# A five-stage attention and RWKV pipeline on one core: additions moved from GpSimd's datapath into accumulating DMA transfers, and a new order of the jobs

## The chip, the core and the metric

The kernel runs on one core of a Trainium2 chip. A core has five engines that run their own instruction streams and wait for each other by semaphores: TensorE (PE), VectorE (DVE), ScalarE (ACT), GpSimd (POOL) and SyncE (SP); 16 DMA engines move data. The metric is the device time of one launch in microseconds, the median of the runs. The kernel before: 1928.44 us (three runs, 1928.34 to 1928.8).

## The reference

32 samples of 128 x 512 floats pass two blocks, each with the second input `ctx_2048` beside it. The first takes a sample as 128 channels by 512 positions (`conv1x1` is a product with a 128 x 128 matrix and a bias, `inorm` a normalisation over the positions):

```python
Mn = conv1x1(Wn, bn, inorm(x_c));  Mm = conv1x1(Wm, bm, inorm(x_s))
A  = softmax(einsum('bct,bcs->bts', Mn, Mm))
x  = conv1x1(Wo, bo, einsum('bcs,bts->bct', conv1x1(Wl, bl, x_s), A)) + x_c
```

The second is an RWKV block (embedding E = 512, H = 32 heads of 16, sequence 128):

```python
xa = ln(x);  sx = concat(state[:, 1:2] - xa[:, :1], xa[:, :-1] - xa[:, 1:])
xxx = einsum(tanh((xa + sx * maa_x) @ maa_w1), maa_w2)      # five mixings
xk, xw, xv, xr, xg = xa + sx * (maa_stack + xxx)            # the sum that the change moves
w = exp(-exp(time_decay + tanh(xw @ td_w1) @ td_w2))
r, k, v = xr @ Wr.T, xk @ Wk.T, xv @ Wv.T;  g = silu(xg @ Wg.T)
for t: a = k_t v_t^T;  out_t = r_t (u * a + s);  s = a + w_t * s
x1 = x + groupnorm(out) * g @ Wo.T
xc = ln(x1);  xk2, xr2 = xc + sx2 * ffn_maa_k, xc + sx2 * ffn_maa_r
return x1 + sigmoid(xr2 @ Wfr.T) * (relu(xk2 @ Wfk.T)**2 @ Wfv.T)   # and this last sum
```

## The kernel before, in words

The work on it is cut into jobs, and the program is 36 steps of software pipelining: in step s every engine works on up to five samples at once, `b0` (sample s, attention), `b1` (mixing and projections), `b2` (the recurrence), `b3` (group norm, output projection, second layer norm), `b4` (feed-forward end). The order of the jobs on each engine is written out by hand in the five `step` functions; nothing is reordered at run time. A job waits for semaphore counts (`Steps.count`) of the jobs that it needs, then the engine goes on with the next one in its list. PSUM banks are dealt out in a ring by the order in `FRONT_JOBS` and `BACK_JOBS`.

The recurrence of one sample is eight units on DVE, `wkv_outer` (the product of `vrep` and `kT` into `S`, L595), `wkv_scan` (L604) and `wkv_read` (L613). After each unit PE sums over the state, `wkv_sum` (L1101). `S` and `vrep` have two buffers, so the outer product of unit u waits for the sum of unit u - 2; POOL copies the initial state of a unit into `S` (`wkv_s0`, L446), also after the sum of unit u - 2. SP loads `vrep` (512 KB, from DRAM, with each row repeated for 16 partitions) once a unit.

The mixing goes: PE multiplies (`mid_M`, L1057), ACT adds the stack in PSUM (`mid_bias`, L806), DVE multiplies by `sx` into `xf` (`mid_mix`, L570), POOL adds `xa` into `xf` (`mid_add`, L430), and PE projects `xf` (`mid_P`, L974: `Wv`, `Wk`, `Wr`, `Wg`; `mid_D1`, L1078, for w). `xf` has three buffers for the five mixings, in the order v, w, k, r, g. At the end of a sample DVE multiplies into `rr` (`fin_y`, L668), POOL adds `x1` (`fin_out`, L460) and ACT's queue stores `rr` (`fin_store`). POOL also computes the reciprocal roots (`rstd_of`, L400 and L402; the one on `hrs` takes longest) and the product `rku` (`wkv_rk`, L436).

Of the kernel before, what the change touches and what calls it, by code (L numbers as in the profile page):

```python
# [18 lines left out]
ALU = mybir.AluOpType  # L19
# [54 lines left out]
def run(step):  # L74
# [7 lines left out]
    "Mn:0 Mm:0 W1:1 S0:0 Wt:1 S1:0 S2:0 Mv:1 Mw:1 S3:0 Mk:1 Mr:1 Vp:1 Mg:1 D1:1 V:0 T0:0 T1:0 "  # L82
    "T2:0 T3:0 D2:1 E2:1 O:0 Kp:1 Rp:1 G:1 Tx:0").split())]
BACK_JOBS = [(j, int(lag)) for j, lag in (x.split(":") for x in (
    "FV:4 Tg:3 Wo:3 Tx2:3 FK:3 C:2 FR:3").split())]
# [3 lines left out]
def build(nc, x_c, x_s, state, params, att_w, big_w, maa_w1, maa_w2, td_w1, td_w2, out, v_dram):  # L89
    with ExitStack() as ctx:  # L90
# [109 lines left out]
        v_stored = sem("v_stored")  # L200
        out_stored = sem("out_stored")
# [10 lines left out]
        dve_att = Steps(sem("dve_att"), "stats aggr nm mx0 mx1 mx2 ri0 mx3 ri2 ri1 ri3 xin xst xag nm1")  # L212
        dve_mid = Steps(sem("dve_mid"), "sx xx mv mw mk mr s0m s0c mg g")
# [3 lines left out]
        act_att = Steps(sem("act_att"), "xn yn Mn Mm p0 p1 p2 n0 n1 p3 n2 n3 v T0 T1 T2 T3 xhat")  # L217
        act_mid = Steps(sem("act_mid"), "xa tn tx vT dt ez k th r")
        act_mix = Steps(sem("act_mix"), "bv bw br bk bg")
# [56 lines left out]
        def _(sp):  # L276
# [64 lines left out]
            def step(s, on):  # L341
                b0, b1, b2, b3, b4 = on
                if b0: load_st1(b0[0], b0[2])
                if b2: load_vrep(b2[0], b2[2], 4)
                if b2: load_vrep(b2[0], b2[2], 5)
                if b0 and b0[0] + 1 < NB: load_x(b0[0] + 1, 1 - b0[2])
                if b2: load_vrep(b2[0], b2[2], 6)
                if b2: load_vrep(b2[0], b2[2], 7)
                if b1: load_vrep(b1[0], b1[2], 0)
                if b1: load_st0(b1[0], b1[2])  # L350
                if b1: copy_xres(*b1)
                if b1: load_vrep(b1[0], b1[2], 1)
# [8 lines left out]
        def _(eng):  # L361
# [54 lines left out]
            def mid_xa0(n, m, p):  # L416
                v0 = held(eng, regs[0], 16 * (m + 1))
                v1 = held(eng, regs[1], dve_mid.count("xx", n - 1))
                v2 = held(eng, regs[2], pool_mid.count("fg", n - 1))
# [3 lines left out]
                eng.wait_ge(pool_mid.sem, v2)  # L423
# [34 lines left out]
            def fin_out(n, m, p):  # L458
                eng.wait_ge(dve_fin.sem, dve_fin.count("y", n))
                po.tensor_tensor(rr[:, :], rr[:, :], x1[:, :], ALU.add).then_inc(pool_fin.sem, 1)  # L460

            def step(s, on):
                b0, b1, b2, b3, b4 = on
                if b3: wkv_s0(*b3, 6)
                if b4: tail_xc20(*b4)
                if b2: mid_add(*b2, 4)
                if b3: wkv_s0(*b3, 7)
                if b1: att_rstd1(*b1)
                if b1: mid_xa0(*b1)
# [20 lines left out]
        def _(eng):  # L490
# [35 lines left out]
            def att_xin(n, m, p):  # L526
# [25 lines left out]
            def mid_shift(n, m, p):  # L552
# [3 lines left out]
                                  ALU.subtract).then_inc(dve_mid.sem, 1)  # L556
                eng.wait_ge(dve_mid.sem, dve_mid.count("sx", n))
# [21 lines left out]
            def mid_s0(n, m, p):  # L579
# [3 lines left out]
                ve_.tensor_reduce(s0m[:, :], s, X, ALU.add).then_inc(dve_mid.sem, 1)  # L583
                eng.wait_ge(dve_mid.sem, dve_mid.count("s0m", n))
# [59 lines left out]
            def tail_x1(n, m, p):  # L644
                eng.wait_ge(pe_tail.sem, pe_tail.count("Wo", n))
                eng.wait_ge(xres_copied[p], 16 * (m + 1))
                eng.wait_ge(pool_fin.sem, pool_fin.count("out", n - 1))
                ve_.tensor_tensor(x1[:, :], bank_of("Wo")[:, :], xres[:, p, :], ALU.add).then_inc(dve_tail.sem, 1)
                eng.wait_ge(dve_tail.sem, dve_tail.count("x1", n))
                ve_.bn_stats(st62[:, :], x1[:, :]).then_inc(dve_tail.sem, 1)  # L650
                v0 = held(eng, regs[0], dve_tail.count("st", n))
# [18 lines left out]
            def step(s, on):  # L670
                b0, b1, b2, b3, b4 = on
                if b3: wkv_read(*b3, 7)
                if b1: att_rstd1(*b1)

                if b2: wkv_outer(*b2, 0)
                if b0: att_stats(*b0)
                if b2: wkv_scan(*b2, 0)
                if b2: mid_gate(*b2)
                if b2: wkv_read(*b2, 0)
                if b0: att_rstd(*b0)  # L680

# [9 lines left out]
                if b0: att_max(*b0, 0)  # L691
# [561 lines left out]
```

## Time and profile before

| | |
|---|---|
| median of the runs | 1928.44 us |
| the profiled execution's own time | 1927.65 us |
| its span, first to last instruction | 1925.7 us |
| busy, share of the span: PE, DVE | 94%, 93% |
| busy: ACT, POOL | 63%, 57% |
| chain that ended last: DVE, issue, PE, POOL | 54%, 28%, 8%, 8% |
| mean granted TensorE clock | 0.973 |

A busy share is an average over the span, with the filling and draining of the pipeline in it. An instruction's duration runs from its start to its end; the next one on the same engine can begin a little before that end, so for the pace of an engine the starts are compared. A number in brackets at the end of a row is the time the engine was idle before it, and what ended it.

### The profile page before, as it was taken

Reading aid. Unit: us, or ns where it says so; the run is one execution under the profiler, and the core shown is the slowest. Engines: PE = TensorE matmul, PEld = TensorE weight load, DVE = VectorE, ACT = ScalarE, POOL = GpSimd, SP = SyncE. Lnnn points to the kernel's source line nnn. Section 1 sums busy time; section 2 is a strip of 40 time slices with the busy share of each in tenths; the row PEclk is TensorE's granted clock in tenths of the full one; section 3 lists DMA queues with packets and bytes.
Section 4 is the critical chain, followed back from the end, with each engine's and each line's share of the span. In section 5 each row is a group of like instructions: output and inputs, shape, how many; then the busy total and the mean of one; then the engine's idle time right before and its main releaser. Section 6 shows DMA issues by size and latency. Waiting matters only on the chain.

```text
span 1925.7 us, 34674 instructions
## 1 busy us (share of the span) xinstructions
PE 1811.8 (94%) x12356; PEld 1254.5 (65%) x12356; DVE 1785.9 (93%) x2084; ACT 1206.5 (63%) x2849; POOL 1104.6 (57%) x822
## 2 busy tenths in 40 slices
PE   5889999999999999999999999999999999999855
PEld 2666666677666667766666677667667766766633
DVE  3599999999999999999999999999999999999871
ACT  3545766666676666667666666766666666665422
POOL 1256666656666665666666556666655665655431
PEclk8889999999999999999999999999999999999877
DMA  6233333334333333434333343334333333433310
GB/s 236 63 95 97 99 98 97 93 101 106 105 102 98 101 90 101 105 102 106 97 103 92 100 104 102 102 99 103 91 99 105 102 103 96 105 84 95 93 49 11
DMA packets 86202, 189.31 MB, mean 98 GB/s; under 512 B 18800, under 2 KB 35312, under 8 KB 85008
## 3 DMA queue, kind: packets, MB, share of 16 engines
q1 hardware_dynamic: 64528, 170.32, 33.2%
q10 hardware_dynamic: 21504, 16.78, 2.8%
q8 instruction: 100, 1.64, 0.4%
q14 instruction: 70, 0.57, 0.1%
HBM read 161.91 MB, written 16.78 MB: 93 GB/s over the span
## 4 chain that ended last, share of the span: by engine, by line
DVE 54%; issue 28%; PE 8%; POOL 8%; ACT 1%; DVEq 0%; DMA 0%; POOLq 0%; ACTq 0%; SPq 0%
DVE S L604 17%; DVE S L595 11%; POOL hrs L400 4%; DVE S L613 3%; PE bank L974 3%; DVE xr L663 3%; POOL hrs L402 2%; DVE xf L570 2%; POOL S L446 2%; DVE xx L560 2%; PE bank L981 1%; DVE st L532 1%; DVE st L650 1%; DVE xin L529 1%; DVE sx L555 1%
## 5 line engine op out<-in xcount | busy, mean ns | idle before, releaser
L604 DVE TENSOR_TENSOR_SCAN S<-wrep,S 128x1024 f32<-128x1024 f32 x256 | 588.4, 2298 | 2.7 <-ACT wrep L842 0.8
L446 POOL COPY S<-s 128x8 f32<-128x8 f32 x256 | 181.4, 709 | 497.0 <-PE bank L1101 496.8
L430 POOL TENSOR_TENSOR xf<-xf,xa 128x512 f32<-128x512 f32 x160 | 335.2, 2102 | 30.8 <-DVE xf L570 29.1
L595 DVE TENSOR_TENSOR S<-vrep,kT 128x1016 f32<-128x1016 f32 x256 | 337.4, 1318 | 1.3 <-ACT kT L825 1.3
L613 DVE TENSOR_TENSOR S<-S,rT 128x1024 f32<-128x1024 f32 x256 | 316.1, 1235 | 2.3
L806 ACT ACTIVATE bank<-bank,par 128x128 f32<-128x128 f32 x640 | 179.0, 352 | 150.0 <-PE bank L1057 150.0
L400 POOL TENSOR_SCALAR rstd<-mv 128x1 f32<-128x1 f32 (+1 forms) x96 | 129.0, 1344 | 154.7 <-DVE mv L536 83.2
L1101 PE MATMUL bank<-S,slide 128*32 128x256 f32 x2048 | 167.1, 398 | 46.9 <-DVE S L613 46.9
L402 POOL TENSOR_TENSOR hrs<-hrs,mhalf 128x32 f32<-128x32 f32 x32 | 177.4, 5542 | 2.7
L757 ACT ACTIVATE xhat<-xin,nmr,rstd 128x512 f32<-128x512 f32 x32 | 26.1, 815 | 210.5 <-DVE nmr L502 210.5
L1008 PE MATMUL bank<-probT 128*128 128x512 f32 x256 | 134.9, 611 | 7.6 <-ACT prob L769 6.8
L842 ACT ACTIVATE wrep<-ez 128x1016 f32<-128x1016 f32 x128 | 133.3, 1043 | 0.0
L974 PEld LDWEIGHTS bank<-xk,Wfk 128*128 128x128 f32 x1024 | 121.0, 197 | 17.3 <-issue 13.2
L974 PE MATMUL bank<-xk,Wfk 128*128 128x128 f32 x1024 | 127.1, 284 | 3.8 <-DVE xk L663 3.8
L974 PEld LDWEIGHTS bank<-xf,Wk 128*128 128x128 f32 x1024 | 118.6, 194 | 13.6 <-issue 13.6
L400 POOL TENSOR_SCALAR hrs<-hvar 128x32 f32<-128x32 f32 x32 | 69.5, 2171 | 100.7 <-DVE hvar L631 100.7
L886 ACT ACTIVATE xp<-bank,prev 128x128 f32<-128x128 f32 x256 | 127.1, 496 | 0.0
L974 PE MATMUL bank<-xf,Wv 128*128 128x128 f32 x1024 | 126.3, 284 | 0.0
L974 PEld LDWEIGHTS bank<-xf,Wg 128*128 128x128 f32 x1024 | 116.7, 192 | 12.8 <-issue 12.8
L981 PE MATMUL bank<-Wo,ogT 128*128 128x512 f32 x256 | 122.7, 623 | 2.4 <-DVE ogT L642 2.4
L974 PE MATMUL bank<-xf,Wk 128*128 128x128 f32 x1024 | 124.5, 281 | 0.0
L974 PEld LDWEIGHTS bank<-xf,Wv 128*128 128x128 f32 x1024 | 123.4, 201 | 1.3 <-issue 1.0
(133 smaller groups left out, 3770.1 us busy)
## 6 DMA issues: line engine op xcount, KB each, us to landing
vrep<-v_dram SPq DMA_DIRECT2D x256, 512.0 KB
xc<-x_c SPq DMA_DIRECT2D x32, 256.0 KB, 6.4
xs<-x_s SPq DMA_DIRECT2D x32, 256.0 KB, 7.1
v_dram<-vT ACTq DMA_DIRECT2D x32, 256.0 KB, 6.1
xres<-xin SPq DMA_DIRECT2D x32, 256.0 KB, 5.9
out<-rr ACTq DMA_DIRECT2D x32, 256.0 KB, 6.3
Wv<-big_w SPq DMA_DIRECT2D x1, 1024.0 KB, 7.4
Wk<-big_w SPq DMA_DIRECT2D x1, 1024.0 KB, 9.4
```

The costliest lines, as they stand in the source:

```text
L400: po.tensor_scalar(rs, var, EPS, None, ALU.add).then_inc(own.sem, 1)
L402: po.tensor_tensor(rs, rs, mhalf[:, 0:rs.shape[1]], ALU.pow).then_inc(own.sem, 1)
L430: po.tensor_tensor(xf[:, b, :, :], xf[:, b, :, :], xa[:, :, 1:P + 1], ALU.add).then_inc(pool_mid.sem, 1)
L446: po.tensor_copy(S[:, u % 2, :, 0], s0[:, p, k:k + UJ]).then_inc(pool_wkv.sem, 1)
L595: ve_.tensor_tensor(S[:, u % 2, :, 1:P], vrep[:, u % 2, :, 0:P - 1], k, ALU.mult).then_inc(dve_wkv.sem, 1)
L604: ve_.tensor_tensor_scan(s, wrep[:, u % C, :, :].rearrange("p j t -> p (j t)"), s, 0.0, ALU.mult, ALU.add).then_inc(dve_wkv.sem, 1)
L613: ve_.tensor_tensor(s, s, rT[:, p, u % C, :].unsqueeze(1).broadcast_to([P, UJ, P]), ALU.mult).then_inc(dve_wkv.sem, 1)
L806: last = sc.activation(ps, ps, ACT.Identity, bias=col("maa_stack", c, MIX.index(f)))
L974: last = pe.matmul(ps[:, o * P:(o + 1) * P], w[:, c, o * P:(o + 1) * P], src[:, c, :], start=(c == 0), stop=(c == C - 1))
L981: last = pe.matmul(bank_of(job)[:, :], src[:, c, :], w[:, c, :], start=(c == 0), stop=(c == C - 1))
L1008: pe.matmul(bank_of(f"S{t}")[:, :], Mn[:, t * P:(t + 1) * P], Mm, start=True, stop=True).then_inc(pe_att.sem, 1)
L1101: last = pe.matmul(bank[SUM_BANK][32 * g:32 * g + 32, 2 * P * half:2 * P * (half + 1)], ones, S[:, u % 2, g:UJ:4, :], start=(c == 0), stop ...
```

## The change

1. `mid_add` and `fin_out` are no longer POOL tensor instructions. Each is a DMA issued from POOL's queue with `accum_op=ALU.add`, from `xa` into `xf` (five a sample) and from `x1` into `rr` (one a sample). Each kind has a semaphore of its own (`xa_added[f]`, `x1_added`), which counts 16 for a landed transfer.
2. Whoever waited for POOL's counter waits for these: PE's projections and `D1`, ACT's `mid_xa` (for all five, before it overwrites `xa`), DVE's `tail_x1` and ACT's `fin_store` (for the last addition).
3. Functions that issued two or more dependent instructions are cut into single jobs: `att_stats` | `att_aggr`, `att_xin` | `att_xst` | `att_xag`, `mid_shift` | `mid_xx`, `mid_s0` | `mid_s0c`, `tail_x1` | `tail_st` | `tail_ag`, `tail_mix` by half, `att_norm`, `att_proj`, `att_M`, `att_T`, `fin_kr` | `fin_kk`, `fin_rr` | `fin_rs`.
4. Every engine's list is in a new order, and the step is cut at another place: the recurrence's units 0 to 3 are now in the step of `b2` and the scan of unit 4 and units 5 to 7 in that of `b3`; `x1` and what follows belongs to `b4`. The rings of PSUM banks and the counters follow.

```diff
-    "Mn:0 Mm:0 W1:1 S0:0 Wt:1 S1:0 S2:0 Mv:1 Mw:1 S3:0 Mk:1 Mr:1 Vp:1 Mg:1 D1:1 V:0 T0:0 T1:0 "
+    "O:1 D2:2 E2:2 G:2 Rp:2 Kp:2 Tx:1 W1:1 Mn:0 Mm:0 Wt:1 V:0 S0:0 Mv:1 Mw:1 S1:0 S2:0 S3:0 Mk:1 "
...
+        xa_added = {f: sem(f"xa_added_{f}") for f in MIX}
+        x1_added = sem("x1_added")
...
             def mid_add(n, m, p, i):
                 f, b = ORDER[i], i % 3
+                eng.wait_ge(pool_const, CONSTS)
                 eng.wait_ge(dve_mid.sem, dve_mid.count(f"m{f}", n))
-                po.tensor_tensor(xf[:, b, :, :], xf[:, b, :, :], xa[:, :, 1:P + 1],
-                                 ALU.add).then_inc(pool_mid.sem, 1)
+                eng.dma_start(xf[:, b, :, :], xa[:, :, 1:P + 1], accum_op=ALU.add).then_inc(xa_added[f], 16)
...
             def fin_out(n, m, p):
+                eng.wait_ge(pool_const, CONSTS)
                 eng.wait_ge(dve_fin.sem, dve_fin.count("y", n))
-                po.tensor_tensor(rr[:, :], rr[:, :], x1[:, :], ALU.add).then_inc(pool_fin.sem, 1)
+                eng.dma_start(rr[:, :], x1[:, :], accum_op=ALU.add).then_inc(x1_added, 16)
...
             def tail_x1(n, m, p):
-                eng.wait_ge(pool_fin.sem, pool_fin.count("out", n - 1))
+                eng.wait_ge(x1_added, 16 * n)
...
             def mid_xa(n, m, p):
-                eng.wait_ge(pool_mid.sem, pool_mid.count("fg", n - 1))
+                for f in MIX:
+                    eng.wait_ge(xa_added[f], 16 * n)
...
             def mid_P(n, m, p, f, job, name):
-                eng.wait_ge(pool_mid.sem, pool_mid.count(f"f{f}", n))
+                eng.wait_ge(xa_added[f], 16 * (n + 1))
...
             def mid_D1(n, m, p):
-                eng.wait_ge(pool_mid.sem, pool_mid.count("fw", n))
+                eng.wait_ge(xa_added["w"], 16 * (n + 1))
```

What the new lists do to the rows is shown at three places. The first is POOL, from the long root on `hrs` on; `S<-s` is the copy of a unit's initial state, `DMA xf<-xa` the new form of the mixing's addition. Before:

```order
L400 TENSOR_SCALAR hrs<-hvar 128x32
L402 TENSOR_TENSOR hrs<-hrs,mhalf 128x32
L446 COPY S<-s 128x8
L430 TENSOR_TENSOR xf<-xf,xa 128x512 x2
L446 COPY S<-s 128x8 x2
L460 TENSOR_TENSOR rr<-rr,x 128x512
L430 TENSOR_TENSOR xf<-xf,xa 128x512 x2
```

Now:

```order
L401 TENSOR_SCALAR hrs<-hvar 128x32
L403 TENSOR_TENSOR hrs<-hrs,mhalf 128x32
L454 TENSOR_TENSOR xp<-st,par 128x8
L445 COPY S<-s 128x8
L430 DMA xf<-xa 128x4x128
L435 TENSOR_TENSOR rku<-rT,kT 128x512
L430 DMA xf<-xa 128x4x128
L460 DMA rr<-x 128x512
L423 COPY xa<-st 128x4
L445 COPY S<-s 128x8
L430 DMA xf<-xa 128x4x128 x3
```

The copy ahead of the first DMA is that of unit 3, the first DMA is v's, the one behind `rku` w's, and the last three are r's, g's and k's.

The second is PE, from `FV` (`Wfv,kk`) to the output projection `Wo`. `tx,w` and `txg,w2g` are the mixing products, `S,slide` the sum of a unit. Before:

```order
L981 MATMUL bank<-Wfv,kk 128x512 x4
L1008 MATMUL bank<-probT 128x512
L1057 MATMUL bank<-tx,w 128x128 x8
L1101 MATMUL bank<-S,slide 32x256 x4
L986 MATMUL bank<-ident,oc 128x128 x4
L974 MATMUL bank<-xf,Wv 128x128 x16
L1101 MATMUL bank<-S,slide 32x256 x4
L981 MATMUL bank<-Wo,ogT 128x512 x4
```

Now, beginning with the sum of unit 1:

```order
L1130 MATMUL bank<-S,slide 32x256 x4
L1012 MATMUL bank<-Wfv,kk 128x512 x4
L1086 MATMUL bank<-tx,w 128x128 x8
L1086 MATMUL bank<-txg,w2g 128x128 x4
L1017 MATMUL bank<-ident,oc 128x128 x4
L1130 MATMUL bank<-S,slide 32x256 x4
L1005 MATMUL bank<-xf,Wv 128x128 x16
L1107 MATMUL bank<-xf,tw 128x128 x4
L1012 MATMUL bank<-Wo,ogT 128x512 x4
```

The projection of v stands behind the sum of unit 2, and w's product `xf,tw` directly behind it.

The third is DVE around `x1` (the first residual and its statistics), from the read of one unit to the next. Before:

```order
L648 TENSOR_TENSOR x<-bank,xres 128x512
L650 BN_STATS st<-x 128x6
L654 BN_AGGR mv<-st 128x2
L583 TENSOR_REDUCE s0m<-s 128x4
L585 SCALAR_TENSOR_TENSOR s<-s0m,s 128x64
L570 TENSOR_TENSOR xf<-bank,sx 128x512
L613 TENSOR_TENSOR S<-S,rT 128x1024
```

Now:

```order
L659 TENSOR_TENSOR x<-bank,xres 128x512
L624 TENSOR_TENSOR S<-S,rT 128x1024
L606 TENSOR_TENSOR S<-vrep,kT 128x8x127
L663 BN_STATS st<-x 128x6
L615 SCALAR_TENSOR_TENSOR S<-wrep,S 128x1024
L531 SCALAR_TENSOR_TENSOR xin<-bank,bo,xc 128x512
L669 BN_AGGR mv<-st 128x2
L591 TENSOR_REDUCE s0m<-s 128x4
L536 BN_STATS st<-xin 128x6
L624 TENSOR_TENSOR S<-S,rT 128x1024
```

Between two rows that depend on each other there is now at least one that does not.

## Rows read from the trace of the kernel before

**Rows 1.** 1000 us: length, busy PE, PEld, DVE, ACT, POOL; PE clock; DMA share
```profile
500.00:1500.00 1000.00, 987.45 (x6896) 686.49 (x6895) 989.71 (x1161) 672.48 (x1587) 620.13 (x446) 1.00 0.38 100
```
**Rows 2.** PE's timeline over a step (start us, duration us, ...), last row one step later
```profile
994.49 3.70 PE L981 MATMUL bank<-Wfv,kk 128*128 128x512 f32 x8
998.02 1.02 PE L1008 MATMUL bank<-probT 128*128 128x512 f32 x2
998.98 1.16 PE L1057 MATMUL bank<-tx,w 32*128 32x128 f32 x16
1000.07 0.64 PE L1101 MATMUL bank<-S,slide 128*32 128x256 f32 x8
...
1000.64 0.66 PE L986 MATMUL bank<-ident,oc 128*128 128x128 f32 x4
1001.13 3.74 PE L974 MATMUL bank<-xf,Wv 128*128 128x128 f32 x32
...
1009.00 1.15 PE L1057 MATMUL bank<-txg,w2g 32*128 32x128 f32 x8
...
1023.33 3.74 PE L974 MATMUL bank<-xf,Wr 128*128 128x128 f32 x32
1027.00 0.64 PE L1101 MATMUL bank<-S,slide 128*32 128x256 f32 x8
1027.57 3.84 PE L974 MATMUL bank<-xf,Wg 128*128 128x128 f32 x32
1032.08 0.64 PE L1101 MATMUL bank<-S,slide 128*32 128x256 f32 x8 [0.67 <-DVE S L613]
1032.65 3.84 PE L974 MATMUL bank<-xk,Wfk 128*128 128x128 f32 x32
...
1088.57 1.60 PE L974 MATMUL bank<-xk,Wfk 128*128 128x128 f32 x12
```
**Rows 3.** DVE's timeline in the same step
```profile
1009.87 0.69 DVE L650 BATCH_NORM_STATS2 st<-x 128x6 f32<-128x512 f32 x1
1010.67 0.18 DVE L654 BATCH_NORM_AGGREGATE mv<-st 128x2 f32<-128x6 f32 x1
...
1014.35 2.29 DVE L604 TENSOR_TENSOR_SCAN S<-wrep,S 128x1024 f32<-128x1024 f32 x1
...
1017.81 2.20 DVE L595 TENSOR_TENSOR S<-vrep,kT 128x1016 f32<-128x1016 f32 x1
...
1025.07 1.21 DVE L595 TENSOR_TENSOR S<-vrep,kT 128x1016 f32<-128x1016 f32 x1
1026.19 0.69 DVE L663 TENSOR_TENSOR xk<-xk,xp 128x512 f32<-128x512 f32 x1
1026.80 1.76 DVE L663 TENSOR_TENSOR xr<-xr,xp 128x512 f32<-128x512 f32 x1
```
**Rows 4.** POOL's timeline in the same step
```profile
1014.64 1.99 POOL L446 COPY S<-s 128x8 f32<-128x8 f32 x1 [2.42 <-PE bank L1101]
...
1016.74 2.19 POOL L430 TENSOR_TENSOR xf<-xf,xa 128x512 f32<-128x512 f32 x1
1019.92 0.20 POOL L446 COPY S<-s 128x8 f32<-128x8 f32 x1 [0.98 <-PE bank L1101]
...
1026.29 1.72 POOL L436 TENSOR_TENSOR rku<-rT,kT 128x512 f32<-128x512 f32 x1
```
**Rows 5.** DMA issues on the page: the store of v (KB, median us to landing)
```profile
v_dram<-vT ACTq DMA_DIRECT2D x32, 256.0 KB, 6.1
```
**Rows 6.** The transfers of out<-rr, 32 of 256 KB each
```profile
DMA to landing us min/median/max: 2.0/6.3/7.1
```
**Rows 7.** The chain that ended last, while the pipeline drains (start, us, what)
```profile
1866.94 1.08 PE bank L1101 x8
1868.02 6.13 PE bank L974 x32
...
1878.59 0.44 PE bank L1119 x4
```

More of the change, by code:

```diff
@@ L210, in units @@
             return " ".join(f"{x}{u}" for u in range(U) for x in text.split())
-        dve_att = Steps(sem("dve_att"), "stats aggr nm mx0 mx1 mx2 ri0 mx3 ri2 ri1 ri3 xin xst xag nm1")
-        dve_mid = Steps(sem("dve_mid"), "sx xx mv mw mk mr s0m s0c mg g")
+        dve_att = Steps(sem("dve_att"), "stats aggr nm mx0 ri0 mx1 mx2 mx3 ri2 ri1 ri3 xin xst xag nm1")
+        dve_mid = Steps(sem("dve_mid"), "sx xx mv mw mk mr mg s0m s0c g")
         dve_wkv = Steps(sem("dve_wkv"), units("a s q"))
@@ L700, in step @@
                 if b3: tail_gn(*b3)
[L701 removed]
                 if b2: wkv_scan(*b2, 3)
[L703 to L705 removed]
+                if b0: att_rinv(*b0, 3)
+                if b1: mid_mix(*b1, 2)
                 if b2: wkv_read(*b2, 3)
                 if b3: tail_gate(*b3)
[L708 removed]
+                if b4: fin_y(*b4)
                 if b2: wkv_outer(*b2, 4)
[L711 removed]
@@ L880, in tail_xc2 @@
                 eng.wait_ge(pe_fin.sem, pe_fin.count("FR", n - 1))
-                for i, dst in enumerate((xk2, xr2)):
-                    for c in range(C):
-                        ps = bank_of("Tx2")[:, c * P:(c + 1) * P]
-                        sc.activation(dst[:, c, :], ps, ACT.Identity,
-                                      bias=here[:, i, 1, c:c + 1], scale=here[:, i, 0, c:c + 1])
-                        last = sc.activation(xp2[:, i, c, 1:P + 1], ps, ACT.Identity,
-                                             bias=prev[:, i, 1, c:c + 1], scale=prev[:, i, 0, c:c + 1])
-                    last.then_inc(act_tail.sem, 1)
+                dst, label = ((xk2, "xk"), (xr2, "xr"))[i]
+                for c in range(C):
+                    ps = bank_of("Tx2")[:, c * P:(c + 1) * P]
+                    sc.activation(dst[:, c, :], ps, ACT.Identity,
+                                  bias=here[:, i, 1, c:c + 1], scale=here[:, i, 0, c:c + 1])
+                    last = sc.activation(xp2[:, i, c, 1:P + 1], ps, ACT.Identity,
+                                         bias=prev[:, i, 1, c:c + 1], scale=prev[:, i, 0, c:c + 1])
+                last.then_inc(act_tail.sem, 1)
             def fin_kr(n, m, p):
@@ L905, in fin_store @@
             def fin_store(n, m, p):
-                eng.wait_ge(pool_fin.sem, pool_fin.count("out", n))
+                eng.wait_ge(x1_added, 16 * (n + 1))
                 dst = out[n] if isinstance(n, int) else out[bass.ds(n, 1)].rearrange("o p f -> (o p) f")
@@ L1009, in att_S, with att_T @@
                           start=True, stop=True).then_inc(pe_att.sem, 1)
-            def att_T(n, m, p):
+            def att_T(n, m, p, c):
                 eng.wait_ge(act_att.sem, act_att.count("n3", n))
-                for c in range(C):
-                    eng.wait_ge(*bank_free(f"T{c}", n))
-                    transposes(f"T{c}", lambda t: prob[:, t, c * P:(c + 1) * P]).then_inc(pe_att.sem, 1)
+                eng.wait_ge(*bank_free(f"T{c}", n))
+                transposes(f"T{c}", lambda t: prob[:, t, c * P:(c + 1) * P]).then_inc(pe_att.sem, 1)
             def att_O(n, m, p):
+                eng.wait_ge(act_att.sem, act_att.count("v", n))
                 eng.wait_ge(*bank_free("O", n))
```

305 lines of the change are left out of this document (161 added, 144 removed).

## The prediction, made before the changed kernel was run

> **What bounds the kernel now.** I read the windows view first, because the page's shares mix filling, steady part and draining. In 1000 us of the steady part PE is busy 987 and DVE 990 [rows 1]; both look full, ACT and POOL do not, and DMA is at 0.38. So the page's "DVE 54%" of the chain does not yet say which engine has room. PE's timeline does: `Wfk` starts at 1032.65 and in the next step at 1088.57, so a step takes 55.92 us, and in it PE has one wait, on DVE, ahead of the sum of unit 7 [rows 2]. The block `Wg` takes 1032.08 - 1027.57 = 4.51 from start to start, the equal block `Wr` 3.67; PE therefore loses 0.84 us a step and fills the other 55.08. On DVE's timeline no row of the step carries an idle time. DVE sets the pace, and PE stands 0.84 us (1.5%) behind it. Whatever DVE gains beyond 0.84 us a step is not paid out.
>
> **POOL's additions and DVE.** On POOL's timeline an addition runs from 1016.74 to 1018.93 [rows 4]. DVE's outer product started at 1017.81 and took 2.20, where the one at 1025.07 took 1.21 [rows 3]: 0.99 us, once a step, and it ends 1.08 after the addition does. This addition goes, so 0.99 goes. The sum for `xr` takes 1.76 beside 0.69 for `xk`, but it runs beside POOL's `rku`, 1026.29 to 1028.01 [rows 3, 4]; `rku` stays and only moves, so I count between 0 and 1.07 for it.
>
> The Trainium skill, "SBUF — State Buffer", section "Who interferes with whom", says that a DVE instruction with two SBUF inputs and a GpSimd instruction that reads SBUF take a shared port in turns, whole instructions at a time. The two pairs of rows agree. The same page's box on GpSimd's queue speaks against the change, and I come back to it.
>
> **The splitting and the new order on DVE.** A row that needs the one before it starts late: `mv` starts 0.11 after `st` ends, while an independent row starts 0.09 before its predecessor's end (1025.07 + 1.21 against 1026.19) [rows 3]. That is 0.20 lost. In the list before I count ten such pairs a step (three of statistics like this one, `x1`/`st`, `xin`/`st`, `sx`/`xx`, `s0m`/`s0c`, one outer/scan and two scan/read); in the new one there is one, outer/scan of unit 6. Nine pairs at 0.1 to 0.2 are 0.9 to 1.8; I take 1.3. DVE's step then is 55.92 - 0.99 - 1.3 = 53.6, or 52.6 if `rku` misses `xr`. The multiplications themselves stay. DVE gets 2 to 3 us of room, and PE becomes the bound.
>
> **PE.** It issues the same matmuls. Its floor is 55.08 if the blocks join as before. In the new list 28 waits are doubled up at the start of a block, 24 before (the four transposes of `prob` now wait for two each). What one costs has no row of its own; from below it is 0, from above 0.1 (3.84 for a block of 32 against 3.74 [rows 2]). I take 0.25 for four: 55.33, a gain of 0.59 us a step.
>
> **The price: how long an accumulating transfer takes.** The trace has none. From below, 256 KB alone took 2.0 us to land [rows 6]. The other 256 KB transfers mostly run beside a load of `vrep` and take 6.1 and 6.3, 7.1 at most [rows 5, 6]; `v_dram` is, like `xf`, cut into runs of 512 bytes. An accumulating one reads its target too: from above 7.1 plus another lone 2.0, 9.1. An addition on POOL took 2.19 [rows 4], so each of the six gets later by 0 to 7. DMA engines are 38% busy [rows 1], so a transfer is as often alone as beside `vrep`; I take 5.5, between 2.0 + 2.0 and 7.1.
>
> The Trainium skill, "DMA: Bandwidth & Descriptors", section "Anatomy of one DMA — SWDGE (gpsimd) path", gives 2.0 us plus bytes over 436 GB/s for a transfer from this queue, which would be an estimate of 2.6 us here. By it no wait below would bite and the time would be that of the forecast; the rows of 6.1 and 6.3 do not agree once `vrep` is in flight.
>
> Where it matters is read off the new lists. v's DMA stands on POOL behind the copy for unit 3, which waits for the sum of unit 1. On PE, from the end of that sum to `Wv`: `FV` 3.53, the products for k and r 1.09, for g about 1.08, `oc` 0.49, the sum of unit 2 0.57 (starts to starts, [rows 2]), together 6.76. Of it 0.45 goes on the semaphore and the copy (0.20 [rows 4]) and 0.1 on the way back. A landing within 6.2 us costs nothing; each us more is paid by PE in every step. Queued behind `Wv` on PE are w's product, `Wo`, two transposes and the sum of unit 3, for which DVE's unit 5 waits, so nothing makes it up.
>
> The second deadline is `rr`: DVE may write `x1` only when the last addition has read it. Between `fin_y` and `x1` DVE now has an outer product, two mixings and a scan, 1.12 + 2 x 0.6 + 2.2 = 4.5, and its room of 2 to 3: 6.5 to 7.5. w has about 3.7 more than v on PE but is issued some 3 us later, behind `rku`. g, last out of DVE, has the two last transposes, `O` and `D2` before it, about 10 us. All four bite at nearly the same length of 6.2 to 7, v's first. Copies of initial state that sit behind these issues on POOL had room before (one waited 2.42 for PE [rows 4]).
>
> **Filling and draining.** In the draining, `Wfk`'s 6.13 and `Wfr` stand between the last sum at 1866.94 and the transpose at 1878.59, 11.65 [rows 7]. In the new list only `C` does; `Wfk` stands ahead of the sum instead, where it overlaps one read (1.2). Saved: about 7.6, given back: about 4.9. The last addition becomes a transfer, +1 to +3, and in the filling three additions lie in a chain, +2 each at most. I take 0, from -6 to +6.
>
> **The sum.** Own time of the profiled execution 1927.65 (span 1925.7 and 1.95 around it), less 30 steady steps x 0.59 = 17.7, plus 0: 1910.0. The median of the runs is 0.8 above the profiled one: 1910.8, I say 1910.
>
> **Rivals.** First, the transfer is too long (slower). If it lands after 8 us, v's projection starts 1.8 late in each step, the step is 55.33 + 1.8 = 57.13, and 30 x 1.21 = 36 more than before: 1964. It decides from a landing of 6.8 us (6.2 + 0.59). For it: every 256 KB row beside `vrep` is at 6.1 or more, and reading the target comes on top. Against: `vrep` for unit 4 is nearly through when v is issued. A second way to the same place: POOL prepares the transfer and is held up by DVE. Its copy of 8 elements took 1.99 where another took 0.20, under a scan that ran from 1014.35 to 1016.64 [rows 3, 4]. If an issue is held up likewise, 5.5 + 1.8 = 7.3 and the time is 1928 + 30 x 0.5 = 1943. This is where the Trainium skill's "SBUF — State Buffer", section "SBUF: two separate sides", stands against the change: GpSimd locked out of the port cannot write the descriptors of its DMA. It says so for another kind of DVE instruction than the scan, and the trace shows only the copy. I give both 0.32.
>
> Second, no change: the landing is 6.2 to 6.9, or PE's block starts eat the 0.84. Within 4 us of 1928; 0.10.
>
> Third, more than forecast: PE's block starts cost nothing extra and the draining gains its 6: 30 x 0.84 = 25, plus 6: 1897. 0.13, which leaves 0.45 for the forecast.
>
> **How the numbers follow.** 0.2% (about 4 us) is what can be told from no change. Faster: 0.45 + 0.13 = 0.58; same 0.10; slower 0.32. The range begins at 1895, just under the third rival, and ends at 1964, a landing of 8 us; a landing of 9 (1994) is left out. The forecast's own range is 1902 to 1920.
>
> **What would show it.** Right: in the steady part a step of about 55.3; DVE with idle time of 2 us a step and no outer product of 2.2; PE with no idle ahead of `Wv`; transfers landing in 4 to 6 us. Wrong: PE idle ahead of `Wv` or `D1` for a landed DMA; DVE waiting at `x1` for the addition; POOL's rows under a scan stretched to 2 us right at the issues. If DVE still has no idle time, my reading of the collisions is wrong.

## The result, and the profile after

The changed kernel takes 2146.99 us (median of 4 runs, 2141.38 to 2151.93); beside it the kernel before took 1928.62. The ratio is 1.113, 95% interval 1.1115 to 1.1143: 11.3% slower, far outside the predicted range of 1895 to 1964.

The windows view of the kernel after: the same 1000 us as [rows 1], and 16 us inside one step. Columns as in [rows 1]. A DMA packet's whole time is counted in the stretch in which it starts, so a short stretch can show a share over 1.

```profile
500.00:1500.00 1000.00, 895.33 (x6046) 639.76 (x6048) 838.97 (x1016) 583.99 (x1392) 400.19 (x389) 0.93 0.53 111
...
1002.00:1006.00 4.00, 4.00 (x20) 1.54 (x20) 4.00 (x4) 0.51 (x2) 0.00 (x0) 1.00 1.24 173
1006.00:1010.00 4.00, 0.47 (x8) 0.28 (x6) 3.96 (x9) 1.96 (x5) 2.47 (x5) 0.88 0.89 182
1010.00:1014.00 4.00, 0.95 (x4) 0.95 (x5) 2.97 (x3) 0.00 (x0) 2.08 (x1) 0.50 0.58 129
1014.00:1018.00 4.00, 4.00 (x30) 4.00 (x29) 0.00 (x0) 0.00 (x0) 0.00 (x0) 0.76 0.56 150
```

PE fell from 987 busy to 895, DVE from 990 to 839. Neither is full, so it is a wait that sets the pace. PE's timeline shows which (start, duration, ..., idle before and what ended it):

```profile
991.19 3.84 PE L1005 MATMUL bank<-xf,Wv 128*128 128x128 f32 x32
994.87 1.06 PE L1107 MATMUL bank<-xf,tw 128*128 128x128 f32 x8
...
1013.05 5.18 PE L1005 MATMUL bank<-xf,Wg 128*128 128x128 f32 x32 [6.57 <-DMA xf<-xa]
1018.07 0.60 PE L1017 MATMUL bank<-ident,sq 128*128 128x128 f32 x4
1018.60 0.64 PE L1130 MATMUL bank<-S,slide 128*32 128x256 f32 x8
```

There is no wait ahead of `Wv` and none ahead of w's product (there, PE waits for a landing twice in the program, 3.7 us in all). PE stands 6.57 us ahead of `Wg`, for the landing of g's addition. The granted clock then goes from 1.00 (2.4 GHz) to 0.50 (1.2 GHz) while PE does nothing, and `Wg` takes 5.18 where it took 3.84 before [rows 2]. DVE, one unit of the recurrence ahead, next stands for the sum behind `Wg`. Its timeline has one long wait in the step (the others are of 1.1 us at most), and one long outer product:

```profile
986.87 2.51 DVE L606 TENSOR_TENSOR S<-vrep,kT 128x1016 f32<-128x1016 f32 x1
...
995.08 1.20 DVE L606 TENSOR_TENSOR S<-vrep,kT 128x1016 f32<-128x1016 f32 x1
...
1019.37 1.22 DVE L606 TENSOR_TENSOR S<-vrep,kT 128x1016 f32<-128x1016 f32 x1 [6.40 <-PE bank L1130]
```

POOL's timeline has the issues, and `rku` at a new place:

```profile
985.62 1.37 POOL L430 DMA_DIRECT2D xf<-xa  x1
986.52 1.77 POOL L435 TENSOR_TENSOR rku<-rT,kT 128x512 f32<-128x512 f32 x1
...
995.72 0.87 POOL L460 DMA_DIRECT2D rr<-x  x1 [6.16 <-DVE rr L683]
...
997.42 3.89 POOL L430 DMA_DIRECT2D xf<-xa  x3 [0.50 <-DVE xf L578]
```

The DMA view of 996 to 1015 (out<-in, queue, count, KB, median us to landing; `rr<-x` is the addition of `x1`):

```profile
xf<-xa POOLq DMA_DIRECT2D x3, 256.0 KB, 14.8
rr<-x POOLq DMA_DIRECT2D x1, 256.0 KB, 4.0
v_dram<-vT ACTq DMA_DIRECT2D x1, 256.0 KB, 8.5
```

The three transfers of `xf` are those of r, g and k, issued at 997.42, 998.18 and 998.93. They land after 8.7, 14.8 and 20.4 us: at 1006.1, 1013.0 and 1019.4, some 6.6 us apart. The median of the three is g's.

The waits and the chain, for the whole span (total, times, longest; then shares of the chain):

```profile
DVE S L606 <- PE bank L1130: 195.2, 27, 9.1
...
PE bank L1005 <- DMA xf<-xa: 180.3, 28, 8.4
```

```profile
PE 63%; DMA 20%; DVE 8%; issue 6%; POOL 2%; ACT 1%; SPq 0%; POOLq 0%; DVEq 0%; ACTq 0%
```

The group of `Wg` on the page (busy us, mean ns of one | idle before it), here and with half of `vrep` (an experiment below):

```profile
L1005 PE MATMUL bank<-xf,Wg 128*128 128x128 f32 x1024 | 186.2, 366 | 180.3 <-DMA xf<-xa 180.3
```

```profile
L1017 PE MATMUL bank<-xf,Wg 128*128 128x128 f32 x1024 | 124.6, 281 | 2.0 <-DMA xf<-xa 2.0
```

A step takes mostly 63 to 65 us, against 55.9. Over 18 whole steps (644.67 to 1802.16) it is 64.3: PE works 57.1 and stands 7.2. Without the stall (half of `vrep`) it works 54.7 of 54.85 a step. So of the 9.4 us between them about 7 is standing, nearly all of it ahead of `Wg`, and 2.4 is matmuls at the lower clock, all of them in `Wg`'s block. Over the whole program: first scan of the recurrence at 91.1 instead of 78.9, last scan to the end 59.0 instead of 62.3, and 211.0 us more between them.

### The profile page after: what moved, and what is told of

Same layout as the page of the kernel before. It is cut to its first block, busy times and chain, and to the rows that moved or that the text cites. A ratio compares the mean times of both kernels' runs of the same rounds, so it can differ in the third digit from the quotient of the medians.

```text
span 2145.6 us, 35090 instructions
## 1 busy us (share of the span) xinstructions
PE 1854.8 (86%) x12356; PEld 1318.0 (61%) x12356; DVE 1736.0 (81%) x2084; ACT 1197.1 (56%) x2849; POOL 823.1 (38%) x822
## 3 DMA queue, kind: packets, MB, share of 16 engines
q0 software_dynamic: 89088, 50.34, 19.7%
## 4 chain that ended last, share of the span: by engine, by line
PE 63%; DMA 20%; DVE 8%; issue 6%; POOL 2%; ACT 1%; SPq 0%; POOLq 0%; DVEq 0%; ACTq 0%
PE bank L1005 26%; DMA xf<-xa 20%; PE bank L1012 10%; PE bank L1037 5%; PE bank L1086 5%; PE bank L1130 4%; DVE S L615 3%; PE bank L1024 3%; PE bank L1017 2%; PE bank L1065 2%; PE bank L1139 2%; PE bank L1030 1%; DVE S L624 1%; DVE ogT L653 1%; DVE rr L683 1%
## 5 line engine op out<-in xcount | busy, mean ns | idle before, releaser
L445 POOL COPY S<-s 128x8 f32<-128x8 f32 x256 | 192.0, 750 | 927.0 <-PE bank L1130 913.7
L606 DVE TENSOR_TENSOR S<-vrep,kT 128x1016 f32<-128x1016 f32 x256 | 346.9, 1355 | 195.5 <-PE bank L1130 195.2
L1005 PE MATMUL bank<-xf,Wg 128*128 128x128 f32 x1024 | 186.2, 366 | 180.3 <-DMA xf<-xa 180.3
L1005 PEld LDWEIGHTS bank<-xf,Wg 128*128 128x128 f32 x1024 | 180.1, 277 | 186.2 <-DMA xf<-xa 185.7
L430 POOL DMA_DIRECT2D xf<-xa x160 | 224.0, 1703 | 61.5 <-DVE xf L578 61.5
L906 ACT ACTIVATE xk<-bank,here 128x128 f32<-128x128 f32 x128 | 59.6, 465 | 291.7 <-PE bank L1017 291.7
L790 ACT ACTIVATE prob<-bank,nmax 128x512 f32<-128x512 f32 x128 | 88.5, 692 | 98.5 <-DVE nmax L521 98.5
L1005 PEld LDWEIGHTS bank<-xk,Wfk 128*128 128x128 f32 x1024 | 120.9, 197 | 20.2 <-DVE xr L678 11.5
L1037 PE MATMUL bank<-probT 128*128 128x512 f32 x256 | 129.1, 607 | 4.4 <-ACT prob L790 4.4
L1005 PEld LDWEIGHTS bank<-xf,Wv 128*128 128x128 f32 x1024 | 123.5, 201 | 14.4 <-issue 11.3
L1005 PEld LDWEIGHTS bank<-xf,Wr 128*128 128x128 f32 x1024 | 116.7, 192 | 12.8 <-issue 12.8
L578 DVE TENSOR_TENSOR xf<-bank,sx 128x512 f32<-128x512 f32 x160 | 106.2, 676 | 21.1 <-PE bank L1005 13.2
```

The costliest lines, as they stand in the source:

```text
L430: eng.dma_start(xf[:, b, :, :], xa[:, :, 1:P + 1], accum_op=ALU.add).then_inc(xa_added[f], 16)
L445: po.tensor_copy(S[:, u % 2, :, 0], s0[:, p, k:k + UJ]).then_inc(pool_wkv.sem, 1)
L606: ve_.tensor_tensor(S[:, u % 2, :, 1:P], vrep[:, u % 2, :, 0:P - 1], k, ALU.mult).then_inc(dve_wkv.sem, 1)
L1005: last = pe.matmul(ps[:, o * P:(o + 1) * P], w[:, c, o * P:(o + 1) * P], src[:, c, :], start=(c == 0), stop=(c == C - 1))
L1037: pe.matmul(bank_of(f"S{t}")[:, :], Mn[:, t * P:(t + 1) * P], Mm, start=True, stop=True).then_inc(pe_att.sem, 1)
```

## The experiments

The theory, from this profile: PE waits for g's landing, and the landing is late because of what r, g and k share and queue behind. Rivals: the new order is at fault, not the transfers; or an accumulating transfer is slow by itself, wherever it stands. This table has the time from issue to landing, from the traces (medians over the 32 samples, us):

| | v | w | r | g | k | x1 |
|---|---|---|---|---|---|---|
| after | 4.3 | 5.5 | 8.9 | 14.9 | 20.2 | 4.0 |
| g first (issued g, r, k) | 4.3 | 5.5 | 14.2 | 8.6 | 19.3 | 3.9 |
| plain copies | 3.0 | 2.8 | 8.7 | 8.7 | 9.3 | 4.2 |
| `xa` contiguous | 3.3 | 3.8 | 8.3 | 9.5 | 12.6 | 3.7 |
| g on POOL | 4.3 | 5.5 | 8.7 | - | 11.9 | 4.0 |
| r on POOL | 4.3 | 5.5 | - | 8.3 | 13.9 | 3.9 |
| half of `vrep` | 4.3 | 5.4 | 6.1 | 7.2 | 8.8 | 3.8 |
| contiguous, g first | 3.3 | 3.7 | 9.2 | 7.4 | 12.3 | 3.7 |
| contiguous, x1 on POOL, g first | 3.3 | 3.8 | 7.2 | 5.8 | 8.1 | - |
| old order | 9.8 | 9.7 | 6.8 | 5.4 | 4.9 | 3.5 |
| old order, contiguous | 8.3 | 8.5 | 5.1 | 5.2 | 4.2 | 3.4 |

A landing costs only what it is over its slack, the time from its issue to the point where its user would start without waiting. In the kernel after that is (medians) 5.6 us for v, 7.1 for w, 8.3 for g and 4.0 for `x1`; where nothing is late it is 13.8 for r and 15.9 for k (half of `vrep`).

**The new order alone.** All six additions on POOL again:

```diff
+BY_DMA = ""
+X1_BY_DMA = False
...
-                eng.dma_start(xf[:, b, :, :], xa[:, :, 1:P + 1], accum_op=ALU.add).then_inc(xa_added[f], 16)
+                if f in BY_DMA:
+                    eng.dma_start(xf[:, b, :, :], xa[:, :, 1:P + 1], accum_op=ALU.add).then_inc(xa_added[f], 16)
+                else:
+                    po.tensor_tensor(xf[:, b, :, :], xf[:, b, :, :], xa[:, :, 1:P + 1],
+                                     ALU.add).then_inc(xa_added[f], 1)
```

> The changed kernel with all six additions back as GpSimd tensor instructions; order and splitting as changed. Theory 1 (the loss is the landing of the transfers: g's lands 14.9 us after its issue, PE waits 6.6 us a step for it): the loss goes, PE is the bound at about 55.3 us a step, 1905 to 1925. Theory 2 (the new order itself costs PE or DVE time): stays above 1950 with a step over 57 us.

1963.03 us, ratio 1.0169 (1.015 to 1.0189). The bounds set for theory 2 were met (over 1950, and steps over 57 from the twelfth on) and theory 1's 1905 to 1925 was not, but the loss is only 35 of the 218 us: the order has a price of its own, and the landing has the rest. Steps are 56.4 and, from the thirteenth on, 58.0. POOL's and DVE's timelines of one step:

```profile
1435.32 6.43 POOL L437 TENSOR_TENSOR xf<-xf,xa 128x512 f32<-128x512 f32 x3
```

```profile
1435.47 3.17 DVE L626 TENSOR_TENSOR_SCAN S<-wrep,S 128x1024 f32<-128x1024 f32 x1 [0.31 <-POOL S L453]
...
1439.15 1.56 DVE L635 TENSOR_TENSOR S<-S,rT 128x1024 f32<-128x1024 f32 x1
1440.64 2.19 DVE L617 TENSOR_TENSOR S<-vrep,kT 128x1016 f32<-128x1016 f32 x1
```

Three additions in a row stretch scan, read and outer product by 0.9, 0.3 and 1.0. `nmr` comes late, and PE waits for ACT's `sq` (54.6 us in all). So the new order, with all its additions on POOL, gains nothing; with five or six of them as transfers that land in time it does (below).

**The transfers alone.** The order and functions of the kernel before, with the additions as transfers:

```diff
-                po.tensor_tensor(xf[:, b, :, :], xf[:, b, :, :], xa[:, :, 1:P + 1],
-                                 ALU.add).then_inc(pool_mid.sem, 1)
+                eng.dma_start(xf[:, b, :, :], xa[:, :, 1:P + 1], accum_op=ALU.add).then_inc(xa_added[f], 16)
```

> The kernel before with only the additions turned into accumulating transfers; old order, nothing split. In the old order g's addition is issued 11 us ahead of Wg and k's 12 us ahead of Wk, v's only 3 us ahead of Wv. Theory 1: v lands after 4.4 us, so Wv waits 1 to 2 us a step and the rest is hidden: 1950 to 2010. Theory 2: the transfers are harmless as such, the time is 1920 to 1935. If any accumulating traffic costs as much as in the changed kernel: above 2100.

2240.24 us, ratio 1.1617 (1.16 to 1.1634). The expectation took 4.4 us for v's landing, as in the new order, and was far off (1950 to 2010). Here v is issued just ahead of a `vrep` load and those of `xc` and `xs`, w just behind them, and they land after 9.8 and 9.7. The waits:

```profile
PE bank L973 <- DMA xf<-xa: 205.5, 32, 7.5
```

The late one is v here, ahead of `Wv`, where its slack is 3.1; g lands in 5.4. DVE also waits for the landing of `x1`, 108.0 us in all. So no addition is slow by itself; the place decides.

**g's transfer ahead of r's.**

```diff
-                if b1: mid_add(*b1, 3)
                 if b1: mid_add(*b1, 4)
+                if b1: mid_add(*b1, 3)
```

> The changed kernel, only g's transfer issued ahead of r's (then k's). Theory 1 (they land one behind the other, about 6 us apart): g lands after 9 us and not 15, the wait ahead of Wg falls from 6.6 to 1 to 2 us and one of 1 to 2 us comes ahead of Wr; 1980 to 2040. If the three share the DMA engines evenly rather than queue: all land at 15 to 20 whichever is first, 2130 to 2160.

2031.90 us, ratio 1.0533 (1.0489 to 1.0577). The first of the three now lands after 8.6, the second after 14.2, with g and r exchanged. The time belongs to the place in the queue, not to g. r's projection comes later than g's, so its 14.2 costs less: steps mostly 58.5 to 61.

**Plain copies.** The transfers of the mixing without the addition (`xf` stays the mixing's first part, overwritten; the mixing's sum is left out):

```diff
-                eng.dma_start(xf[:, b, :, :], xa[:, :, 1:P + 1], accum_op=ALU.add).then_inc(xa_added[f], 16)
+                if f in BY_DMA:
+                    eng.dma_start(xf[:, b, :, :], xa[:, :, 1:P + 1]).then_inc(xa_added[f], 16)
...
```

> The changed kernel with the five transfers into xf as plain copies from the same queue, same pieces and semaphores; the product of the mixing is overwritten and so left out of the result. If the accumulation itself (reading the target, adding) makes the transfers long: g lands under 9 us, 1920 to 1980. If issue, pieces of 512 bytes and sharing with other traffic make it: g still lands at 13 us or more, 2100 to 2150.

1908.36 us, ratio 0.9894 (0.9876 to 0.9912), with steps mostly of 54.9 to 55.0. g lands after 8.7, as the first branch had it, and PE waits 16.2 us for landings in all; the time is under the 1920 to 1980 expected for it. The queue rows of the page (packets, MB, share of 16 engines' span), here and then after:

```profile
q0 software_dynamic: 17408, 50.34, 12.0%
```

```profile
q0 software_dynamic: 89088, 50.34, 19.7%
```

The same bytes in a fifth of the packets. Each kernel has 160 transfers of `xf` and 32 of `x1`. With those of g taken off (below), 72192 packets are left of 89088: (89088 - 72192) / 32 = 528 for a transfer of `xf`, in pieces of 512 bytes. The plain one needs 80: (17408 - 32 x 144) / 160, with 144 for one of `x1` (next run). The first of the three, r's, lands after 8.7 in this form as well; what the plain form changes is that g and k land right behind it and not 6 us apart.

**`xa` contiguous.** The column in front of `xa` goes into a tile of its own, so that a partition's 2 KB are one piece:

```diff
-        xa = sb("xa", [P, C, P + 1])
+        xa = sb("xa", [P, C, P])
+        xb = sb("xb", [P, C])
...
-                ve_.tensor_tensor(sx[:, :, :], xa[:, :, 0:P], xa[:, :, 1:P + 1],
+                ve_.tensor_tensor(sx[:, :, 0], xb[:, :], xa[:, :, 0], ALU.subtract)
+                ve_.tensor_tensor(sx[:, :, 1:P], xa[:, :, 0:P - 1], xa[:, :, 1:P],
...
```

> The changed kernel with the column of the previous state kept in a tile of its own, so that xa (and with it each transfer into xf) is one run of 2 KB a partition instead of four of 512 bytes; DVE gets one more row of 4 elements. Theory 1 (an accumulating transfer costs by its pieces: 464 packets each now, 85 for a plain one): an addition lands in about 3.4 us alone like rr's, g's in 5 to 9 us, PE no longer waits for it: 1900 to 1930. Theory 2 (it costs by the bytes read, added and written): g still lands after 13 us or more, above 2080.

1949.55 us, ratio 1.0109 (1.0094 to 1.0124). Its queue row:

```profile
q0 software_dynamic: 27648, 50.34, 15.2%
```

Against 23040 packets when g's transfers are missing too, that is (27648 - 23040) / 32 = 144 a transfer (the 464 and 85 packets of the expectation are 528 and 80 by these counts). Nine tenths of the loss are gone with the addition still in the transfer: 2147 to 1950. g lands after 9.5, which is still late in most steps (PE waits 39.3 us in 26 places); steps go from 54.8 to 61, and the time is over the 1900 to 1930 expected.

**g's addition on POOL, the other five as transfers.**

Additions not named in `BY_DMA` are POOL's tensor instruction again, at the same place of its list:

```diff
+BY_DMA = "kwvr"
```

> The changed kernel with g's addition alone on GpSimd's datapath, the other five as accumulating transfers in their 512-byte pieces. Theory 1 (only g's landing is late for its user): no wait ahead of Wg, k lands some 9 us after its issue and in time, step 55 to 56.5: 1905 to 1950. If the DMA engines being full holds up vrep and v_dram too: above 1980.

1905.47 us, ratio 0.9875 (0.9859 to 0.9892): steps mostly of 54.8. One addition of six, put back, takes off the whole loss and more, with short pieces for the rest. r still lands after 8.7 and k after 11.9, within their slack; PE waits for landings 9.1 us in the whole program.

**Half of `vrep`.** Each load of `vrep` fetches half (the recurrence's other half of v is left out, as zeros); the transfers stay as they are in the changed kernel:

```diff
-                sp.dma_start(vrep[:, u % 2, :, :].rearrange("p j t -> p (j t)"),
+                sp.dma_start(vrep[:, u % 2, 0:UJ // 2, :].rearrange("p j t -> p (j t)"),
...
```

> The changed kernel with only half of each vrep loaded (256 KB instead of 512; the other half is zeros, so half of the recurrence's input is left out). If the other traffic is what stretches the accumulating transfers (4.3 us alone, 14.9 and 20.2 in the row of three): g lands under 11 us, 2000 to 2080. If it is their own cost, one behind the other: g at 13 us or more, 2110 to 2150.

1898.66 us (one run), steps 54.8 to 54.9, well under the 2000 to 2080 expected: g was to land under 11 us, and lands within its slack of 8.3. The DMA view around the same three issues:

```profile
xf<-xa POOLq DMA_DIRECT2D x3, 256.0 KB, 7.3
...
vrep<-v_dram SPq DMA_DIRECT2D x1, 256.0 KB
v_dram<-vT ACTq DMA_DIRECT2D x1, 256.0 KB, 5.4
```

g goes from 14.9 to 7.2 though nothing of its own queue has changed. The issues take POOL as long as in the kernel after (medians 1.3, 1.8 and 2.4 us for r, g and k in both), so it isn't the issuing that makes the landings late. In the kernel after, the DMA engines' share is 1.24 from 1002 to 1006 and 0.89 from 1006 to 1010, with 0.53 as the mean, but 0.58 and 0.56 in the 8 us behind that, while g and k are still not landed. The queues' packets say more. From 1003 to 1006 POOL's queue moves 763 packets, with 9 of SP's queue and 203 short ones of ACT's (the store of v) beside it. From 1006 to 1013, beside `vrep`, `xc` and `xs`, it moves 307, and SP's queue 346, whose packets are over five times as long (0.92 MB against 0.15). From 1013 to 1019.4 it is 161 against 214. The Trainium skill, "DMA: Bandwidth & Descriptors", section "Queues, rings and completion order", says that each DMA engine takes its queues in turns, packet by packet, which would let a queue with short packets fall behind one with long ones. The counts and the landings agree; no view here shows the turns of a single engine.

So it is the sharing with SP's loads that spreads r, g and k 6.6 us apart; with half of `vrep` they land 1 to 2 apart. The run doesn't separate `vrep` from `xc` and `xs`: with half of `vrep` the three are through, or nearly, when those two are issued.

**r's addition on POOL**, the mirror of the run with g's:

```diff
+BY_DMA = "kwvg"
```

> Short pieces of 512 bytes as in the changed kernel, but r's addition runs on POOL, so that g's transfer has none in front of it in its queue; the load of vrep and the store of v stay. Theory A, g waits behind r in the queue: g lands 8 to 10 us after its issue, as r did (8.7), PE waits 3 us or less for it, the step is 57 to 60 us and the time 1960 to 2030. Theory B, the sharing with vrep and the store of v alone makes g late: g still lands after 13 us or more, the step stays over 62 us and the time over 2080.

1921.60 us, ratio 0.9967 (0.9949 to 0.9984). g, now with no transfer of `xf` in front of it, lands after 8.3 (once after 14.8, in a step of 63.9) and k, in the second place, after 13.9: theory A on the landing, not B. The price was put too high, though (1960 to 2030 was expected). One step shows why: g is issued at 1019.44 and lands 8.1 later, at 1027.55, and PE's timeline has

```profile
1027.60 3.84 PE L1016 MATMUL bank<-xf,Wg 128*128 128x128 f32 x32
```

without an idle time before it. g may take 8.3 us from its issue, and each us more is paid. (In the kernel after: 14.83 - 6.57 = 8.26.)

**Two remedies, three times.** First contiguous pieces with g's transfer ahead of r's:

```diff
-        xa = sb("xa", [P, C, P + 1])
+        xa = sb("xa", [P, C, P])
...
-                if b1: mid_add(*b1, 3)
                 if b1: mid_add(*b1, 4)
+                if b1: mid_add(*b1, 3)
```

> As e5_contiguous_xa, with g's transfer issued ahead of r's. If e5 leaves a wait ahead of Wg, this takes it away: PE's floor, 1895 to 1915. If e5 leaves none: the same as e5 within 0.3%.

1899.51 us, ratio 0.9843 (0.9827 to 0.986). g lands after 7.4, r after 9.2.

Then contiguous pieces with g's addition on POOL:

```diff
+BY_DMA = "kwvr"
...
+        xa = sb("xa", [P, C, P])
```

> The two remedies together: xa contiguous, and g's addition on POOL. In the theory (the price is what stands behind one another between r's issue and g's landing) each alone already takes the stall from PE, so a second one has nothing left to remove: step 54.6 us as with contiguous pieces and g first, time 1893 to 1902. If POOL's addition of g beside DVE costs something that the transfer doesn't, it is 1903 to 1908, as with g alone on POOL. If shorter pieces also give time elsewhere (x1, the fill), it is under 1890.

1890.40 us, ratio 0.9804 (0.9787 to 0.982): a little under what was expected. Last, contiguous, g first (both edits as above), and `x1`'s addition back on POOL:

```diff
+BY_DMA = "kwvrg"
+X1_BY_DMA = False
```

> xa contiguous, g first, and the last residual's addition back on POOL, all five of the mixings by transfer. Does the last addition's transfer bring anything? Theory: on POOL it runs 2.2 us beside DVE and stretches at most one DVE instruction by 1 us, while DVE has over 1 us of room: 1898 to 1905, no different from the kernel with all six as transfers (1899.5). Rival: the slot right behind w's transfer makes POOL start it later, x1 waits, and the time is 1910 to 1930.

1885.70 us (1884.74 to 1889.48), ratio 0.9783 (0.9769 to 0.9798), the fastest version, 2.2% under the kernel before. No difference had been expected; it is 14 us in the medians, 9 between the two profiled executions. Of these 9, 4.8 are between the scans and 3.7 behind the last one. The transfer of `x1` is issued 1.7 us ahead of the three (995.72 and 997.42 above) and loads the same stretch: without it g lands after 5.8 instead of 7.4, k after 8.1 instead of 12.3. It also has a deadline of its own, at which it lands: its slack is 4.0 us and its landing 3.7 to 4.0. With `x1` as a transfer there is still a step of 59.4 and two of 55.5, and in that of 59.4 DVE waits 3.9 us at `x1` for the last addition's landing, as the waits show:

```profile
DVE x L672 <- DMA rr<-x: 4.8, 4, 3.9
```

Without the transfer of `x1` the step is 54.6 from the third to the last but one. Windows and chain of the fastest:

```profile
500.00:1500.00 1000.00, 1000.00 (x7061) 703.48 (x7062) 976.39 (x1211) 680.29 (x1629) 453.29 (x460) 1.00 0.53 127
```

```profile
PE 92%; DVE 3%; issue 2%; ACT 1%; POOL 1%; DMA 0%; SPq 0%; POOLq 0%; DVEq 0%; ACTq 0%
```

PE is busy in all of the 1000 us: what is left to gain is in its matmuls.

**Contiguous pieces in the old order.**

```diff
-                po.tensor_tensor(xf[:, b, :, :], xf[:, b, :, :], xa[:, :, 1:P + 1],
-                                 ALU.add).then_inc(pool_mid.sem, 1)
+                eng.dma_start(xf[:, b, :, :], xa[:, :, :], accum_op=ALU.add).then_inc(xa_added[f], 16)
```

> The order and the functions of the kernel before, its six additions as accumulating transfers, xa contiguous. With 512-byte pieces this order cost 66 to 67 us a step: v's transfer landed after 9.8 us and PE waited up to 7.5 ahead of Wv. Theory, the transfers need both short landings and an order with room for them: the old order has v's addition as the last thing ahead of Wv, about 3.5 us of slack against a landing of 6 to 8 (v.1 of the steps runs beside a load of vrep), so 2.5 to 4.5 us a step over 55: 58 to 61, time 1990 to 2080. Rival, the pieces alone were the fault: the step is at most 56 and the time at most 1940.

2188.64 us, ratio 1.1342 (1.1323 to 1.1361). Short landings of v (8.3, from 9.8) help it by 52 us and no more. The waits:

```profile
DVE xf L570 <- PE bank L975: 187.2, 32, 7.0
...
PE bank L975 <- DMA xf<-xa: 153.2, 30, 6.2
```

The rival (pieces alone) is out. The time is above what the theory expected too: besides the 5 us ahead of `Wv` (153.2 / 30), DVE's next mixing waits for PE (187.2 in all) and its `x1` for the last addition's landing (104.8). Pieces, order and traffic all have to fit; in these runs neither the new order nor the transfers gain without the other.

## Why the prediction was wrong

The step that failed is the price of a landing and where it was applied: "so a transfer is as often alone as beside `vrep`; I take 5.5", one figure for six transfers, from a mean DMA share of 0.38. That is w's landing (5.5) and more than v's (4.3) and `x1`'s (4.0), but far under the other three. Three of the six stand 0.75 us apart in one queue, right behind `x1`'s, with `vrep` and the store of v in flight, where the share reaches 0.9 to 1.2 in place of 0.38, and they take 8.9, 14.9 and 20.2. g's 14.9 is 6.6 over its slack of 8.3, and that, not v, is what PE pays for in nearly every step (28 waits). The upper end, 9.1, was the sum for one such transfer. That three go at once was in the list of POOL's instructions ahead of the prediction (the row with x3) and was never priced.

Point by point:

- **g's deadline.** "About 10 us", against 8.3 measured. Near enough, but with 14.9 it decides. Which addition bites first was argued by deadline alone ("v's first"), and "nearly the same length of 6.2 to 7" does not fit the 10 given for g. v's slack was put at 6.2 and is 5.6; v landed 1.3 us inside it.
- **The deadline of `rr`.** 6.5 to 7.5 was forecast, 4.0 measured: DVE comes to `x1` sooner than was counted. The landing of 4.0 just meets it (13 waits, 6.5 us in all). Had it taken the 5.5 of the sum, DVE would have stood at `x1` in every step; this term was wrong and did no harm, by luck.
- **The first rival** had the right mechanism, at the wrong place and price: a landing too long, but at g, 6.6 over its deadline, not 1.8 at v. It also left out PE's clock after the wait, about 2 us a step. The sum closes: 180.3 us of waits for landings ahead of the projections and 61.6 that `Wg`'s matmuls take longer (186.2 - 124.6), less 36.0 that the steps gain where nothing is late (1784.4 between first and last scan before, 1748.5 with half of `vrep`), are 206; 211.0 were lost.
- **The second way of that rival**, POOL held up in its issue by DVE, is not what happened. The rows of the issues are 1.3 to 2.4 us long, the same whether the landing is late or not, and v lands after 4.3 (5.8 at most).
- **DVE.** Ten dependent pairs to one and no addition beside it: 53.6 was forecast; with half of `vrep` DVE is busy 978.53 of 1000, 53.7 of a step of 54.85. The sum comes out near that, but the idle time is 1.2 a step and not the 2 to 3 of room that the prediction named (its own figures, 55.33 less 53.6 or 52.6, give 1.7 to 2.7). In its parts the term doesn't hold: `rku`, counted as 0 to 1.07 of gain, left `xr` alone and now stretches the outer product of unit 3 (2.51 against 1.20). A POOL instruction that is moved takes its collision along. This agrees with the Trainium skill, "SBUF — State Buffer", section "Who interferes with whom".
- **PE's floor.** 55.33 was forecast, 54.6 to 54.9 measured wherever no landing is late, less even than the 55.08 that it started from. The doubled waits cost nothing that can be seen; why PE's matmuls of a step are busy 54.7 and not 55.3 us was not looked into.
- **The plain copies** come to 1908.4, close to the forecast of 1910, and that is luck: their landings are not 5.5 but 2.8 to 9.3. The steps gain 29.1 us in place of 17.7, and filling and draining lose 5.9 in place of 0 (11.1 more and 5.2 less).
- **The edges.** 0 was taken, with +6 as the bound: 12.2 more in the filling and 3.3 less in the draining, +8.9, more than the bound. In the fastest version it is 88.3 + 56.5 against 78.9 + 62.3, +3.6.
- **The formula** of the Trainium skill, "DMA: Bandwidth & Descriptors", section "Anatomy of one DMA — SWDGE (gpsimd) path" (2.6 us as an estimate for such a transfer), fits a plain copy alone (2.7 at the least), not an accumulating one in short pieces alone (4.2 at the least), and says nothing of a queue.

Shown: g's landing is what costs (taking it away, halving the traffic, or shortening the pieces each removes the cost); the place in the queue decides who is late (g and r exchanged, r taken away); the sharing with SP's loads, together with the short pieces, sets the spacing (halving `vrep`, or plain copies beside a whole `vrep`, each take it away). Only argued: how the DMA engines divide themselves between the queues. Not tried: the short pieces with `x1`'s addition alone on POOL.

## What to carry to other kernels

A transfer's landing is priced where it is issued: which transfers stand ahead of it in its queue, and what the DMA share is in those ten microseconds, not on average. Of several operations turned into transfers, price the last of a burst, and put the one with the nearest deadline first. Work out each one's slack from the new order, not only that of the one which looks tightest. Before an addition is moved to DMA, make its source and target contiguous, so that pieces are long; and check that the order leaves each landing its time.

## What the runs showed of the hardware

- An accumulating transfer of 256 KB within SBUF, with little beside it, lands after 4.2 to 4.3 us in pieces of 512 bytes and 3.2 to 3.3 in pieces of 2 KB; a plain copy of the same 512-byte pieces after 2.7 to 3.0. They make 528, 144 and 80 packets.
- The Trainium skill, "DMA: Bandwidth & Descriptors", section "Why small descriptors are slow (HBM only)", says that transfers within SBUF don't suffer from short pieces. For accumulating ones the runs differ: 4.3 against 3.3 alone, and 14.9 against 9.5 in the second place beside `vrep`.
- The issue of such a transfer is a row of 1.3 to 2.4 us on POOL in short pieces, 0.85 to 1.6 in long ones, 0.75 to 1.0 for the plain copy; rows that follow each other overlap. Busy time over 160 issues is 224.0, 150.6 and 125.2 us (1.4, 0.9 and 0.8 each), against 335.2 (2.1 each) for the additions before.
- Beside long packets of SP's queue, POOL's queue of 512-byte packets moved 307 packets in 7 us (SP's 346), where it moved 763 in 3 us beside 9 of SP's and 203 short ones of ACT's.
- In a wait of 6.6 us PE's granted clock fell from 1.00 to 0.50, and the 32 matmuls behind it took 5.18 us instead of 3.84.
